# The end of attention and the start of the last feed-forward part in hand-written engine lists

## The reference

```python
x = x + 0.5 * ffn(layernorm(x))
x = x + attn(layernorm(x))
x = x + 0.5 * ffn(layernorm(x))

def ffn(z):     # 256 -> 768 -> 256, weights rounded to fp8 e4m3 and scaled
    return ((silu(z @ gate * gs) * (z @ up * us)) @ down) * ds

def attn(z):    # 16 heads of 128
    q, k, v = (silu(causal_conv4(z @ W)) for W in (Wq, Wk, Wv))   # k also / sqrt(128)
    a, b = sigmoid(z @ Wa + ba), sigmoid(z @ Wb + bb)
    for each token:
        err = S @ k - v
        S = a * S - b * outer(err, k)
        o = S @ q
    return (layernorm(o) * ln_w + ln_b) * sigmoid(z @ Wg) @ Wo
```

## Time and profile before

| | |
|---|---|
| median of 3 runs | 2467.68 us (2467.63 to 2468.91) |
| the profiled execution | 2468.06 us |
| its span, first to last instruction | 2466.3 us |
| mean granted PE clock | 0.987 |
| PE busy | 2357.2 us, 96% |
| DVE busy | 2017.2 us, 82% |
| ACT busy | 1817.0 us, 74% |
| POOL busy | 1818.9 us, 74% |
| chain that ended last, by engine | PE 81%, DVE 6% |

### The profile page before, as it was taken

One profiled execution on the slowest core, in us unless ns is written; L12 is line 12 of the kernel. 1 busy time (PEld: TensorE's weight loads), 2 busy tenths in 40 slices (PEclk: granted clock), 3 DMA queues, 4 the chain that ended last, 5 costly groups with the idle time before them and its releaser, 6 DMA issues.

```text
span 2466.3 us, 64137 instructions
## 1 busy us (share of the span) xinstructions
PE 2357.2 (96%) x24496; PEld 1827.6 (74%) x24496; DVE 2017.2 (82%) x4246; ACT 1817.0 (74%) x3566; POOL 1818.9 (74%) x1973
## 2 busy tenths in 40 slices
...
DMA packets 72833, 103.59 MB, mean 42 GB/s; under 512 B 21456, under 2 KB 33744, under 8 KB 72400
## 3 DMA queue, kind: packets, MB, share of 16 engines
q1 hardware_dynamic: 72528, 99.48, 15.9%
...
## 4 chain that ended last, share of the span: by engine, by line
PE 81%; DVE 6%; issue 1%; POOL 1%; ACT 1%; DVEq 0%; POOLq 0%; ACTq 0%
PE a_bank L1887 25%; PE a_bank L1867 7%; PE a_bank L1676 5%; PE a_bank L1690 5%; PE a_bank L1829 5%; PE a_bank L1828 4%; PE a_bank L1811 3%; PE a_bank L1722 3%; PE a_bank L1736 3%; PE a_bank L1734 3%; PE a_bank L1957 3%; DVE a_prod L1140 3%; PE a_bank L1759 2%; PE a_bank L1846 2%; PE a_bank L1749 2%; PE a_bank L1699 2%
## 5 line engine op out<-in xcount | busy, mean ns | idle before, releaser
L1887 PE MATMUL a_bank<-k_z,k_kqv 128*128 128x512 f16 x2304 | 597.9, 380 | 10.7 <-DVE a_kb L1233 4.2
L1462 ACT ACTIVATE a_inv<-a_bank 128x512 f16<-128x512 f32 x640 | 383.4, 599 | 216.9 <-PE a_bank L1736 201.5
L1164 DVE TENSOR_TENSOR k_y<-a_bank,k_masks 128x256 f16<-128x256 f32 x768 | 318.7, 415 | 134.9 <-PE a_bank L1722 131.1
L1887 PEld LDWEIGHTS a_bank<-k_z,k_kqv 128*128 128x128 f16 x2304 | 197.9, 98 | 139.8 <-DVE a_kb L1233 6.2
L912 POOL TENSOR_TENSOR k_diag<-k_ident,k_bcol 128x512 f32<-128x512 f32 x128 | 133.0, 1039 | 224.1 <-DVE a_prod L1140 209.1
L1233 DVE SCALAR_TENSOR_TENSOR a_kb<-a_bank,k_prm,a_kb 128x511 f32<-128x511 f32 (+2 forms) x384 | 282.7, 737 | 14.6 <-ACT a_kb L1406 14.3
L1233 DVE SCALAR_TENSOR_TENSOR a_vb<-a_bank,k_prm,a_vb 128x511 f32<-128x511 f32 (+2 forms) x384 | 283.7, 739 | 0.1
L1233 DVE SCALAR_TENSOR_TENSOR a_qb<-a_bank,k_prm,a_qb 128x511 f32<-128x511 f32 (+2 forms) x384 | 282.8, 737 | 0.5 <-ACT a_qb L1406 0.3
L1736 PE MATMUL a_bank<-a_inv,k_y 128*128 128x64 f16 x3072 | 271.8, 193 | 3.8 <-DVE k_y L1164 3.8
L1734 PE MATMUL a_bank<-k_y,a_inv 128*128 128x64 f16 x2560 | 236.5, 193 | 5.6 <-DVE k_y L1164 3.1
L1722 PEld LDWEIGHTS a_bank<-a_inv,a_am 128*128 128x128 f16 x3072 | 169.1, 98 | 92.6 <-ACT a_inv L1462 2.0
...
## 6 DMA issues: line engine op xcount, KB each, us to landing
a_decay<-decay_rows SPq DMA_DIRECT2D x128, 258.0 KB, 3.7
...
```

Source lines behind the costliest of these rows:

```text
L1164: nc.vector.tensor_tensor(even(y16[:, j], mb), bank[LEV[par]][:, 0:U * C // 2].rearrange("p (u b m) -> p u b m", u=U, m=mb), masks[:, j].r ...
L1462: nc.scalar.activation(both, bank[LEV[par]][:, :].rearrange("p (two b m) -> p two b m", two=2, m=mb), ACT.Copy).then_inc(m[f"act_lev{par}" ...
L1887: mm = pe.matmul(bank[PJ[j % 2]][:, :], wt, z16[:, zh, k, cols], start=(x == 0), stop=(x == 5))
```

## The change

`tail` goes on all four compute engines. The loop over `step` ends earlier (POOL at step 120, DVE at 119, ACT at 123, PE at 124 as before), and what follows stands in one explicit list per engine, to the middle of the last part's second batch element; `turn(b)` then starts at b = 2 and not 1. `gate_up` becomes `last_gate` and `last_up`. No operation is added, removed or changed, and SP's queue stays as it is. Lists that only write out `step` are left out below.

On POOL:

```diff
-for s in range(-8, STEPS - 4):
-    step(s)
 nc.gpsimd.memset(eps[:, :], EPS).then_inc(f["pool_eps"], 1)
 pool.wait_ge(f["pool_eps"], 1)
+for s in range(-8, STEPS - 7):
+    step(s)
+system_low(STEPS - 7)
 root2(0)
-step(STEPS - 4)
+one(STEPS - 5, 1)
+strengths(STEPS - 5)
+gated(STEPS - 9)
+one(STEPS - 5, 0)
+system16(STEPS - 6)
+first_inverse(STEPS - 6)
+root(STEPS - 8)
+low(STEPS - 9)
+one(STEPS - 5, 3)
+scaled_k(STEPS - 7)
+system_low(STEPS - 6)
+state(STEPS - 7)
+one(STEPS - 5, 2)
...
+first_inverse(STEPS - 3)
+root(STEPS - 5)
+low(STEPS - 6)
+system_low(STEPS - 3)
+one(STEPS - 1, 1)
 root2(1)
-for s in range(STEPS - 3, STEPS):
-    tail(s)
+strengths(STEPS - 1)
+gated(STEPS - 5)
+one(STEPS - 1, 0)
+system16(STEPS - 2)
...
+scaled_k(STEPS - 3)
+system_low(STEPS - 2)
+state(STEPS - 3)
+one(STEPS - 1, 2)
...
+scaled_k(STEPS - 2)
+system_low(STEPS - 1)
+state(STEPS - 2)
+scaled_q(STEPS - 2)
+gated(STEPS - 3)
+hidden_low(0)
+hidden_low(1)
+root2(2)
+root(STEPS - 2)
+low(STEPS - 3)
+scaled_k(STEPS - 1)
+hidden_low(2)
+hidden_low(3)
+hidden_low(4)
 scaled_q(STEPS - 1)
 gated(STEPS - 2)
+hidden_low(5)
+root(STEPS - 1)
 low(STEPS - 2)
-root(STEPS - 1)
 hidden_low(6)
+root2(3)
 hidden_low(7)
 hidden_low(8)
+hidden_low(9)
+hidden_low(10)
 gated(STEPS - 1)
 low(STEPS - 1)
-root2(2)
-hidden_low(9)
-hidden_low(10)
+stream_added(0)
 hidden_low(11)
-stream_added(0)
-root2(3)
-for b in range(1, B):
+hidden_low(12)
+hidden_low(13)
+root2(4)
+hidden_low(14)
+hidden_low(15)
+hidden_low(16)
+stream_added(1)
+hidden_low(17)
+for b in range(2, B):
     turn(b)
```

On DVE:

```diff
-for s in range(-8, STEPS - 4):
+for s in range(-8, STEPS - 8):
     step(s)
...
+mixing(STEPS - 7)
+level(STEPS - 7, 0)
 stats2(0)
-step(STEPS - 4)
+level(STEPS - 8, 5)
+output(STEPS - 10)
+level(STEPS - 7, 1)
+decays(STEPS - 6)
+level(STEPS - 7, 2)
+residual(STEPS - 8)
...
+tap(STEPS - 2, 3, 2)
+level(STEPS - 4, 3)
+tap(STEPS - 2, 3, 3)
+statistics(STEPS - 5)
+aggregated(STEPS - 5)
+level(STEPS - 4, 4)
+mixing(STEPS - 3)
+level(STEPS - 3, 0)
 stats2(1)
-for s in range(STEPS - 3, STEPS):
-    tail(s)
+level(STEPS - 4, 5)
+output(STEPS - 6)
+level(STEPS - 3, 1)
+decays(STEPS - 2)
+level(STEPS - 3, 2)
+residual(STEPS - 4)
+corrected(STEPS - 4)
+system(STEPS - 2)
+level(STEPS - 3, 3)
+statistics(STEPS - 4)
+aggregated(STEPS - 4)
+level(STEPS - 3, 4)
+z_low(0)
+mixing(STEPS - 2)
+level(STEPS - 2, 0)
+new_state(STEPS - 4)
+level(STEPS - 3, 5)
+output(STEPS - 5)
+level(STEPS - 2, 1)
+z_low(1)
+decays(STEPS - 1)
+level(STEPS - 2, 2)
+residual(STEPS - 3)
+hidden(0)
+corrected(STEPS - 3)
+system(STEPS - 1)
+level(STEPS - 2, 3)
+statistics(STEPS - 3)
+aggregated(STEPS - 3)
+hidden(1)
+level(STEPS - 2, 4)
+mixing(STEPS - 1)
+level(STEPS - 1, 0)
+new_state(STEPS - 3)
+level(STEPS - 2, 5)
+output(STEPS - 4)
+level(STEPS - 1, 1)
+stats2(2)
+hidden(2)
+level(STEPS - 1, 2)
+residual(STEPS - 2)
+corrected(STEPS - 2)
+level(STEPS - 1, 3)
+hidden(3)
+statistics(STEPS - 2)
+aggregated(STEPS - 2)
+hidden(4)
+level(STEPS - 1, 4)
+new_state(STEPS - 2)
+hidden(5)
+level(STEPS - 1, 5)
+stats2(3)
+output(STEPS - 3)
+residual(STEPS - 1)
+hidden(6)
 corrected(STEPS - 1)
-hidden(7)
 statistics(STEPS - 1)
 aggregated(STEPS - 1)
+hidden(7)
 hidden(8)
-output(STEPS - 2)
-stats2(2)
 hidden(9)
 scales()
+down_scaled(0)
+output(STEPS - 2)
 hidden(10)
+z_low(2)
+hidden(11)
+stats2(4)
+hidden(12)
+hidden(13)
+hidden(14)
+hidden(15)
+z_low(3)
 output(STEPS - 1)
-hidden(11)
-down_scaled(0)
-z_low(2)
-stats2(3)
-for b in range(1, B):
+hidden(16)
+down_scaled(1)
+hidden(17)
+for b in range(2, B):
     turn(b)
```

On ACT:

```diff
-for s in range(-8, STEPS - 3):
+for s in range(-8, STEPS - 4):
     step(s)
+affine(STEPS - 6)
+acc(STEPS - 2, 3)
+level(STEPS - 4, 2)
 z_normed(0)
-for s in range(STEPS - 3, STEPS):
-    tail(s)
+silu(STEPS - 2, 0)
+silu(STEPS - 2, 1)
+gate(STEPS - 1, 0)
+silu(STEPS - 2, 2)
+level(STEPS - 4, 3)
+silu(STEPS - 2, 3)
+high(STEPS - 6)
...
+affine(STEPS - 5)
+gate(STEPS - 1, 2)
+level(STEPS - 3, 2)
+gate(STEPS - 1, 3)
+z_high(0)
+level(STEPS - 3, 3)
+high(STEPS - 5)
+first_inverse(STEPS - 2)
+z_normed(1)
+level(STEPS - 3, 4)
+normed(STEPS - 4)
+level(STEPS - 2, 0)
+z_high(1)
+kdecayed(STEPS - 2)
+level(STEPS - 3, 5)
+right_side(STEPS - 3)
+level(STEPS - 2, 1)
+first_solution(STEPS - 3)
+affine(STEPS - 4)
+hidden_gate(0)
+level(STEPS - 2, 2)
+level(STEPS - 2, 3)
+hidden_gate(1)
+high(STEPS - 4)
+first_inverse(STEPS - 1)
+level(STEPS - 2, 4)
+normed(STEPS - 3)
+level(STEPS - 1, 0)
+level(STEPS - 2, 5)
+hidden_gate(2)
+hidden_high(0)
+right_side(STEPS - 2)
+level(STEPS - 1, 1)
+first_solution(STEPS - 2)
+affine(STEPS - 3)
+hidden_gate(3)
+hidden_high(1)
+level(STEPS - 1, 2)
+hidden_gate(4)
+level(STEPS - 1, 3)
+hidden_gate(5)
+high(STEPS - 3)
+level(STEPS - 1, 4)
+normed(STEPS - 2)
+hidden_high(2)
+level(STEPS - 1, 5)
+hidden_gate(6)
+right_side(STEPS - 1)
+hidden_high(3)
+first_solution(STEPS - 1)
+hidden_high(4)
 affine(STEPS - 2)
 hidden_gate(7)
 high(STEPS - 2)
+hidden_high(5)
+hidden_gate(8)
+z_normed(2)
+normed(STEPS - 1)
 hidden_high(6)
 hidden_high(7)
-hidden_gate(8)
-normed(STEPS - 1)
-hidden_high(8)
 hidden_gate(9)
-hidden_high(9)
 affine(STEPS - 1)
 hidden_gate(10)
+hidden_high(8)
+z_high(2)
+hidden_high(9)
+hidden_high(10)
+hidden_gate(11)
+hidden_gate(12)
 high(STEPS - 1)
-hidden_high(10)
-z_normed(2)
-hidden_gate(11)
+hidden_gate(13)
 hidden_high(11)
-z_high(2)
-for b in range(1, B):
+z_normed(3)
+hidden_high(12)
+hidden_high(13)
+hidden_gate(14)
+hidden_gate(15)
+z_high(3)
+hidden_high(14)
+hidden_gate(16)
+hidden_high(15)
+hidden_high(16)
+hidden_gate(17)
+hidden_high(17)
+for b in range(2, B):
     turn(b)
```

On PE:

```diff
-def gate_up(x):
+def last_gate(x):
...
+def last_up(x):
+
+    if not 0 <= x < MT * B:
+        return
     need(pe, f["dve_hidden"], x)
     products(bank[PJ[1]], fup16, x, f["pe_up"])
...
-        gate_up(x + MT + j)
+        last_gate(x + MT + j)
+        last_up(x + MT + j)
         if j == 2:
             z_turned(b + 2)
...
 for s in range(-8, STEPS - 3):
     step(s)
-for s in range(STEPS - 3, STEPS):
-    tail(s)
+level_b(STEPS - 3, 2)
+gram_k(STEPS - 2)
+correction(STEPS - 4)
+level_a(STEPS - 3, 3)
+z_turned(0)
+read(STEPS - 4, 0, U // 2)
+read(STEPS - 4, U // 2, U)
+level_b(STEPS - 3, 3)
+level_a(STEPS - 3, 4)
+first_inverse(STEPS - 2)
+gram_q(STEPS - 2)
+update(STEPS - 4)
+level_b(STEPS - 3, 4)
+level_a(STEPS - 2, 0)
+k_turned(STEPS - 2)
+z_turned(1)
+level_b(STEPS - 2, 0)
+level_a(STEPS - 3, 5)
+output(STEPS - 5)
+level_b(STEPS - 3, 5)
+level_a(STEPS - 2, 1)
+v_turned(STEPS - 3)
+state_k(STEPS - 3)
+level_b(STEPS - 2, 1)
+out_turned(STEPS - 4)
+last_gate(0)
+first_solution(STEPS - 3)
+level_a(STEPS - 2, 2)
+last_up(0)
+check_solution(STEPS - 3)
+level_b(STEPS - 2, 2)
+gram_k(STEPS - 1)
+correction(STEPS - 3)
+level_a(STEPS - 2, 3)
+last_gate(1)
+read(STEPS - 3, 0, U // 2)
+read(STEPS - 3, U // 2, U)
+level_b(STEPS - 2, 3)
+last_up(1)
+level_a(STEPS - 2, 4)
+first_inverse(STEPS - 1)
+gram_q(STEPS - 1)
+update(STEPS - 3)
+level_b(STEPS - 2, 4)
+level_a(STEPS - 1, 0)
+last_gate(2)
+level_b(STEPS - 1, 0)
+level_a(STEPS - 2, 5)
+output(STEPS - 4)
+level_b(STEPS - 2, 5)
+level_a(STEPS - 1, 1)
+v_turned(STEPS - 2)
+state_k(STEPS - 2)
+level_b(STEPS - 1, 1)
+last_up(2)
+out_turned(STEPS - 3)
+first_solution(STEPS - 2)
+last_gate(3)
+level_a(STEPS - 1, 2)
+check_solution(STEPS - 2)
+last_up(3)
+level_b(STEPS - 1, 2)
+correction(STEPS - 2)
+last_gate(4)
+level_a(STEPS - 1, 3)
+read(STEPS - 2, 0, U // 2)
+read(STEPS - 2, U // 2, U)
+level_b(STEPS - 1, 3)
+last_up(4)
+last_gate(5)
+level_a(STEPS - 1, 4)
+update(STEPS - 2)
+level_b(STEPS - 1, 4)
+last_up(5)
+last_gate(6)
+level_a(STEPS - 1, 5)
+output(STEPS - 3)
+level_b(STEPS - 1, 5)
+v_turned(STEPS - 1)
+state_k(STEPS - 1)
+last_up(6)
+out_turned(STEPS - 2)
+first_solution(STEPS - 1)
+down(0)
+check_solution(STEPS - 1)
+down(1)
+last_gate(7)
 correction(STEPS - 1)
-down(0)
+down(2)
+last_up(7)
 read(STEPS - 1, 0, U // 2)
 read(STEPS - 1, U // 2, U)
-down(1)
-gate_up(8)
+last_gate(8)
+down(3)
+down(4)
+last_up(8)
+last_gate(9)
+down(5)
 output(STEPS - 2)
-down(2)
-gate_up(9)
 out_turned(STEPS - 1)
-down(3)
-gate_up(10)
-down(4)
+last_up(9)
+last_gate(10)
+z_turned(2)
+last_up(10)
+last_gate(11)
+down(6)
+last_up(11)
+last_gate(12)
+down(7)
+last_up(12)
+last_gate(13)
+down(8)
+last_up(13)
+last_gate(14)
 output(STEPS - 1)
-gate_up(11)
-down(5)
-z_turned(2)
-for b in range(1, B):
+last_up(14)
+z_turned(3)
+last_gate(15)
+down(9)
+last_up(15)
+last_gate(16)
+down(10)
+last_up(16)
+last_gate(17)
+down(11)
+last_up(17)
+for b in range(2, B):
     turn(b)
```

More of the change, by code:

```diff
@@ new lines, in _ @@
+            strengths(STEPS - 5)
[10 more added lines that the diff above has]
+            one(STEPS - 5, 2)
+            strengths(STEPS - 4)
+            scaled_q(STEPS - 7)
+            gated(STEPS - 8)
+            system16(STEPS - 5)
```

241 lines of the change are left out of this document (129 added, 112 removed).

## The result

The changed kernel takes **2429.29 us**, the median of 4 runs (2427.95 to 2429.68), against 2467.65 us for the kernel before in 4 runs on the same chip. The ratio is 0.9843, 95% interval 0.9828 to 0.9858: 38.4 us faster. Forecast were 31.1 us and a time of 2437.0.

What follows compares the result with a forecast made beforehand. PE bounds the kernel, so only its idle and lower-clock time can be won; gains of 6.2 + 13.4 + 5.0 + 2.7 + 4.1, less 0.3, give 31.1 us off 2468.06: 2437.0 us, range 2430 to 2452.

Steps and rivals of the forecast that it cites:

- the 3.5 us "left": PE idle time expected to remain: 1.0 us in step 126, 1.0 in step 127, 1.5 in the drain.
- the floor of 37.7 us: Most that could be won from step 124 on: 30.1 us of PE idle plus 7.6 us of lower clock.
- Step 124: Loses 5.07 us idle and 1.4 us of clock, pays 0.3 us for an insertion: 6.2 us gained.
- The bounded cost of z_normed(0): On ACT in step 124, four activations make level 3 late by 0.3 us, bounds nothing and 1.0.
- The scan: root2(0) pushes POOL's one(123, 1) onto DVE's scan for step 122; 0.3 us lost, at worst 0.9.
- Step 125: ACT sets this step; of 11.42 us idle and 4.5 us of clock all but 2.5 us go: 13.4 us gained.
- the four waits that were followed: PE waits in step 125: z_turned(0) 0.3 us, level_a(4) 0.7, first_inverse(126) 0.8, out_turned(124) 0.6.
- the rival in which it falls in step 125: Transposes and gaps drop PE to 1.2 GHz in step 125, costing 4.5 us: 2441.5 us; chance 16%.
- the low end: Lower limit of the forecast range, 2430 us, from the sum with nothing left idle, 2430.4.
- New head-of-line waits: Tight ACT and POOL lists bring back two or three 3.5 us waits and a clock dip: 2449 us; chance 13%.
- Not doing what it says: Idle time belongs to step 125's chain of levels and returns as many short waits: 2465 us; chance 4%.
- Slower by a round trip per batch: In steps 126, 127 and the drain, 18 batches each wait 2.67 us, 48 us lost: 2485 us; chance 3%.

Runs made afterwards that it cites:

- e6: Changed kernel with POOL's root2(0) put behind one(123, 1) instead of in front; 2428.08 us.
- e7: Changed kernel with the edit of e6, z_high(0) behind level(125, 3) on ACT and update(124) in front of first_inverse(126) on PE; 2428.85 us.
- e3: Changed kernel with the new lists only to the end of step 125, without batch 0's gate and up there, then the old steps and drain; 2440.46 us.
- e4: Changed kernel with the new lists only to the end of step 127, without down(0) and down(1), then the old drain; 2435.81 us.
- e2: Changed kernel with stats2(0), stats2(1), root2(0) and root2(1) put back to their old places; 2445.36 us.
- e9: Changed kernel with z_normed(0) put back at the head of ACT's step 125; 2434.10 us.
- e1: Kernel before with only stats2(0), stats2(1), root2(0) and root2(1) moved to where the change puts them; 2455.71 us in its second run.
- e5: Changed kernel with each last_gate(x), x up to 6, directly in front of its last_up(x), on PE only; 2435.93 us.

## Why the prediction was right in kind and too small

Two terms of the sum failed, both in size and not in kind. The first is the 3.5 us "left" in steps 126, 127 and the drain without a wait that would cause them; the trace has 0.9. The second is the floor of 37.7 us, in which each stall is priced at its idle figure; from start to start the same stalls are 2.1 us longer. The parts follow in the order of the forecast.

**What bounds the kernel: right.** The forecast took the gain as idle time of PE plus time at the lower clock in steps 124 to 127 and the drain, and nothing else. 37.5 of 38.3 us come from there.

**Step 124, 6.2 forecast, 6.5 measured.** 21.40 us became 14.90, which is the whole 5.07 and 1.42. The bounded cost of z_normed(0) on level 3 (nothing to 1.0, taken as 0.3) was nothing to speak of: from the start of the same matmul step 124 takes 14.82 us and its twin 14.76, and PE does not wait in it. stats2(0) and stats2(1) cost nothing visible, as forecast.

**The scan, 0.3 forecast, 0.25 measured** (e6). The mechanism was half wrong, and that a choice between nothing and 0.9 came so near is luck. The forecast read from two maxima that each side pays 0.9 us, and in this meeting only POOL does. The trace of the kernel before could have told it. Its L1000 meets the scan 31 times and takes 2.40 to 2.43 us each time; the other 97 take 1.48 to 1.51. The scan takes 2.05 to 2.08 us in 30 of these meetings, and in all 30 POOL's L979 lies over it for 1 us before L1000 does; in the one where L979 lies over it for only 0.1 us it takes 1.23. One of the 30, POOL and then DVE:

```profile
2201.28 1.05 POOL L979 TENSOR_TENSOR a_zs<-a_z,a_cum 128x512 f32<-128x512 f32 x1
2202.30 2.40 POOL L1000 TENSOR_SCALAR a_gb<-a_gb 128x512 f32<-128x512 f32 x1
```

```profile
2201.36 2.07 DVE L1140 TENSOR_TENSOR_SCAN a_prod<-a_decay,k_diag 128x516 f32<-128x516 f32 x1
```

So the scan pays for L979, which started 0.08 us before it, and L1000 pays for the scan: two meetings, and the change adds only the second. The Trainium skill (Advanced Engine Details and Errata, Mode Summary) names two-port VectorE instructions as those that block GpSimd and by that would charge this meeting nothing; the trace has it at 0.93 us for POOL. The Trainium skill (GPSIMD Engine Reference, Specifications) also names VectorE instructions with two SBUF inputs, which this scan has (a_decay and k_diag), and by that rule the trace agrees.

**Step 125, 2.5 us left forecast, 1.43 measured.** Two of the four waits that were followed are there, nearly to the tenth: 0.7 forecast and 0.69 for level_a(125, 4), 0.8 and 0.74 for first_inverse(126). The other two, z_turned(0) and out_turned(124), did not occur: PE found their inputs ready. The cause given for the first was wrong, as e7 shows (it is not z_high(0)), so its size was luck. ACT is busy 13.06 of 16.00 us, 82%, as forecast. But POOL is busy 15.23 of them, 95%, which the forecast did not count; it is POOL's mask that first_inverse(126) waits for.

**Steps 126 and 127 and the drain, 3.5 us left forecast, 0.9 measured.** Here the forecast left 1.0, 1.0 and 1.5 us without a named wait for each. Steps 126 and 127 have none at all; in the drain there are 0.29 and 0.61. This is the step that failed most: having followed the list and found nearly every input ready, it put a round remainder there all the same. The gain of this part, forecast as 11.8 us, is 13.7 by the traces of e3 and the changed kernel (11.2 by the medians); the drain's, forecast as 4.1, is 6.6 to 6.9, of which 1.7 are the low-clock stretch that only e3 and e4 have there.

**The clock: right.** All 7.6 us came back and the granted clock is 1.00 from step 120 to the last matmul. So the rival in which it falls in step 125 did not happen. That step has five groups of transposes (z_turned twice, k, v and out) and 1.43 us of idle time and still held 2.4 GHz. By the Trainium skill (TensorE: Matmul & The Clock Gate, Part 4: PE-mode transpose) such transposes do not count as busy PE in the same way; with the other matmuls between them this trace does not show it. What e2 and e9 show is that the risk was real: at their waits of 5.00, 5.07 and 2.67 us the clock came down, and each time 2.6 to 2.9 us of clock came on top. The length of a wait alone does not settle it. The wait of 2.67 us in front of L1957 has a low stretch behind it in the kernel before and none in e1, here behind its end at 2279.97:

```profile
2280.00:2290.00 10.00, 10.00 (x92) 7.14 (x93) 5.19 (x15) 5.13 (x11) 5.74 (x8) 1.00 0.01 2
```

And the old drain, whose clock of 1.00 the forecast took as an argument against this rival, falls in e3 and e4 with the same wait of 2.1 us for output(127). That argument was weaker than it looked.

**The floor of 37.7 us: wrong, and with it the low end.** The sum left 6.3 us idle in total and 2.3 are there: 4.0 of the 7.3 us that are missing. The forecast took as the most that could be won what the trace shows as idle, plus the clock. But a matmul's end is modelled, and lies behind the point where the next one could start. In the kernel before, the four matmuls of L1722 start at 2239.89 and the next group at 2245.24, 5.35 us later; in the changed kernel the same pair starts 0.12 us apart. The first row is from the kernel before:

```profile
2239.89 0.28 PE L1722 MATMUL a_bank<-a_inv,a_am 128*128 128x64 f16 x4
```

```profile
2239.18 0.28 PE L1971 MATMUL a_bank<-a_inv,a_am 128*128 128x64 f16 x4
2239.30 0.47 PE L2077 MATMUL a_bank<-a_z,a_qg 128*128 128x128 f32 x2
```

The stall was 5.35 - 0.12 = 5.23 us and its row says 5.07. This wait is 0.16 us longer than its idle figure. The sum over all of them can be had from the two tables: busy time from step 124 to the last matmul was 222.5 - 30.1 = 192.4 us and is now 185.0 - 2.3 = 182.7. That is 9.7 us less for the same instructions, of which 7.6 were counted as clock; 2.1 us were stalls shown as busy time. e5, with nine small waits and a clock of 1.00, shows it without any term for the clock: 4.4 us more idle time, 6.7 us measured and 6.8 by the traces. In e3 the sum needs the clock: by the traces 13.7 us, of which 9.8 are idle and 1.7 clock, and 2.2 are in neither. It does not come to the same for every wait. e2 has only 0.1 us in neither with three waits more than the changed kernel, e5 about 0.25 for each of nine; how the 2.1 us are spread over the waits of the kernel before stays open.

4.0 + 2.1 = 6.1, and the 0.3 charged for the scan lies ahead of this stretch: 31.1 + 6.4 = 37.5, the measured figure. The other 0.8 us are ahead of step 124. Both kernels have the same order there up to step 119, but the changed kernel's first scan already starts 1.4 us earlier, and 1.0 of it is left at step 120, before the meeting with the scan takes 0.3. That is chance of the first phase, as the kernel before shows against itself (2.0 us). It also decides on which side of the low end the time falls: 2430.4 + 2.3 of idle time left - 2.1 of stalls shown as busy is 2430.6, and only the 0.8 us bring the profiled execution below 2430. That the sum was 7 us too small is beyond such chance.

**The other rivals.** New head-of-line waits: none over 0.74 us. Not doing what it says: no. Slower by a round trip per batch: no; the batch pieces show two waits, 0.29 and 0.61 us, in 18 batches, against the 1.7 us for each that this needed.

**What the parts are worth**, by the medians and the traces: norms' places 12 to 13 us alone, or 16 to 18 as the last thing missing; z_normed(0) 4.9 to 6.2; steps 126 and 127 4.6 to 6.8; the drain 6.6 to 6.9; gate and up split, within the new lists, 6.7 to 6.8. They overlap and are not to be added.
